# Routed experts in pairs of half-blocks, each on 64 columns of TensorE

## What is computed

```
logits = x @ router_w + router_b          # [1250, 8]
p, idx = top_k(softmax(logits), 2)        # two experts per node
for e in range(8):                        # w1[e]: [768, 1152], w2[e]: [1152, 768], all fp32
    h = gelu(x @ w1[e] + b1[e])
    y = h @ w2[e] + b2[e]
    out = out + y * gates[:, e:e+1]       # gate 0 where the node did not choose e
```

## Time and profile before

| | |
|---|---|
| median of the runs | 4152.34 µs |
| span of the profiled execution | 4146.1 µs |
| what lies around the span (median less span) | 6.2 µs |
| TensorE matmul busy | 3653.2 µs (88%) |
| DVE, ScalarE, GpSimd busy | 2328.8, 1499.3, 1303.8 µs |
| last stage, `route` | 3416.8 to 3467 µs |
| last stage, `experts` | 3467 to 4146 µs |

### The profile page before, as it was taken

One profiled execution on the slowest core, in us unless ns is written; L12 is line 12 of the kernel. 1 busy time (PEld: TensorE's weight loads), 2 busy tenths in 40 slices (PEclk: granted clock), 3 DMA queues, 4 the chain that ended last, 5 costly groups with the idle time before them and its releaser, 6 DMA issues. The chain is left out here.

```text
span 4146.1 us, 73449 instructions
## 1 busy us (share of the span) xinstructions
PE 3653.2 (88%) x18975; PEld 2492.1 (60%) x18976; DVE 2328.8 (56%) x8246; ACT 1499.3 (36%) x4487; POOL 1303.8 (31%) x1301
## 2 busy tenths in 40 slices
PE   6989999679999897898957779998989997999998
PEld 4656666444444465666646665444556775888787
DVE  5469999977777766777778885640232232101010
ACT  0047777557777421222246663320020100111111
POOL 0045555447777105666636651000000000011010
PEclk9999999879999999999979999999999998999999
DMA  3278888648888427888856761012600008426261
GB/s 117 78 216 268 263 268 269 209 142 268 266 264 270 154 76 248 274 273 273 273 190 196 197 183 70 0 46 91 263 1 27 27 8 325 154 53 248 46 217 58
DMA packets 190279, 711.89 MB, mean 172 GB/s; under 512 B 30132, under 2 KB 52580, under 8 KB 189812
## 3 DMA queue, kind: packets, MB, share of 16 engines
q0 software_dynamic: 102208, 486.37, 37.7%
q1 hardware_dynamic: 87796, 224.24, 15.7%
q10 hardware_dynamic: 192, 0.25, 0.0%
HBM read 777.87 MB, written 33.04 MB: 196 GB/s over the span
## 5 line engine op out<-in xcount | busy, mean ns | idle before, releaser
L635 POOL DMA_INDIRECT X<-fs,near_src x664 | 629.5, 948 | 869.1 <-POOLq L100 436.6
L699 PE MATMUL l_psZ<-X,ident 128*128 128x396 f32 (+3 forms) x2656 | 810.2, 427 | 7.0 <-DMA X<-fs,near_src 6.2
L699 PEld LDWEIGHTS l_psZ<-X,ident 128*128 128x128 f32 x2656 | 498.1, 190 | 195.1 <-DMA X<-fs,near_src 7.2
L696 PE MATMUL l_psZ<-fd,l_spread 128*128 x1328 | 448.9, 418 | 110.4 <-ACT l_spread L612 54.8
L985 PE MATMUL a_psO<-X,a_sel 128*128 128x396 f32 (+1 forms) x1328 | 463.4, 504 | 44.9 <-DVE X L939 44.3
L968 ACT ACTIVATE X<-X,L 128x99 f32<-128x99 f32 x1328 | 373.4, 364 | 131.2 <-DMA X<-fs,pair_src 122.0
L985 PEld LDWEIGHTS a_psO<-X,a_sel 128*128 128x128 f32 x1328 | 242.1, 190 | 265.7 <-issue 105.4
L923 POOL DMA_INDIRECT X<-fs,pair_src x324 | 353.8, 1092 | 139.2 <-issue 82.0
L696 PEld LDWEIGHTS l_psZ<-fd,l_spread 128*128 128x128 f32 x1328 | 234.7, 189 | 193.6 <-issue 173.5
L2522 PEld LDWEIGHTS r_psH<-r_rowsT,ew_w 128*128 128x128 f32 x2916 | 331.7, 193 | 8.4 <-issue 1.5
L662 DVE SCALAR_TENSOR_TENSOR l_zr<-l_psZ,l_attn 128x99 f32<-128x99 f32 x1660 | 330.6, 255 | 8.4 <-issue 6.0
(11 more groups left out here) (504 smaller groups left out, 5317.3 us busy)
## 6 DMA issues: line engine op xcount, KB each, us to landing
ew_w<-in_L_ffn_w SPq DMA_DIRECT2D x54, 3456.0 KB
dsts<-near_rows SPq DMA_DIRECT2D x166, 128.0 KB
room<-in_L_ffn_w SPq DMA_DIRECT2D x8, 2304.0 KB
hw_w<-in_L_ffn_w SPq DMA_DIRECT2D x24, 576.0 KB
X<-fs,near_src POOLq DMA_INDIRECT x664
H<-in_L_ffn_b SPq DMA_DIRECT2D x27, 384.0 KB
X<-in_x SPq DMA_DIRECT2D x2, 3456.0 KB
X<-fs,pair_src POOLq DMA_INDIRECT x332
```

The source lines that it names most:

```text
L635: nc.gpsimd.indirect_dma_start(out=g[:, n % RING, :], out_offset=None, in_=fs, in_offset=bass.IndirectOffsetOnAxis(ap=R.near_src[:, n:n + ...
L696: nc.tensor.matmul(psZ[k][:, a, 0:half], spread[:, j // 4, k, :], R.fd[:, ds(b, 1), lo:hi].squeeze(1), start=True, stop=True)
L699: last = nc.tensor.matmul(psZ[k][:, a, 0:hi - lo], R.ident[:], g[:, j, lo:hi], start=False, stop=True, skip_group_check=True)
```

## The change

Blocks are now half-blocks of 64 slots: MB = 46, and R.slots has MP = 23 columns, in which partitions 0 to 63 belong to half-block i (side 0) and partitions 64 to 127 to half-block i + 23 (side 1). So side 0 goes through half-blocks 0 to 22 and side 1 through 23 to 45, each with weight buffers, and fresh now means that a side's expert differs from that of its block before.

Both products take the rows, or the hidden values, as stationary operand, 64 columns per side, and the weights move: side 0 writes partitions 0 to 63 of PSUM and side 1 partitions 64 to 127, with the two sides' matmuls one after the other in program order. The hidden values thus come out with rows on partitions: DVE adds b1 (which is now loaded as broadcast rows per side), ScalarE applies gelu to the whole tile in one instruction, and nine transposes (`cross`) turn them for the second product. TensorE's order is inner(i), turn(i + 1), outer(i - 1), cross(i).

Each matrix is loaded in thirds with a semaphore each. SyncE's loop pass i waits for each third of inner(i), loads w1 of block i + 1 for both sides, then the bias, then waits for each third of outer(i) and loads w2, then waits for the addition and loads b2, now under the same condition. There are four register loads per pass.

`slots` has two more columns: the nodes with those of the other side replaced by a value out of range. GpSimd scatters each block in two indirect DMAs, one per side, and waits for each to land before the next, since a node may be on both sides. The loops of the other engines are written out.

The diff, cut to its core (indentation shortened by eight inside the scopes; the removed lines of `experts` are those of the kernel printed above):

```diff
-MB = (TOP * NODES - ME) // P + ME
-MSLOTS = MB * P
+SIDE = P // 2
+MB = (TOP * NODES - ME) // SIDE + ME
+MP = MB // 2
+assert MB == 2 * MP
+MSLOTS = MB * SIDE
 KH = MHID // P
+PARTS = 3
...
+    def load_first(self, sp, s, q, e, **how):
+        n = KD // PARTS
+        rows = self.w1[ds(e, 1)].squeeze(0).rearrange("(k p) h -> p k h", p=P)[:, q * n:(q + 1) * n, :]
+        sp.dma_start(self.first[s][:, q * n:(q + 1) * n, :], rows, **how).then_inc(self.s_first[s][q], 16)
+
+    def load_second(self, sp, s, q, e, **how):
+        n = KH // PARTS
+        rows = self.w2[ds(e, 1)].squeeze(0).rearrange("(k p) d -> p k d", p=P)[:, q * n:(q + 1) * n, :]
+        sp.dma_start(self.second[s][:, q * n:(q + 1) * n, :], rows, **how).then_inc(self.s_second[s][q], 16)
+
+    def load_bias(self, sp, s, e, **how):
+        sp.dma_start(self.bias[s * SIDE:(s + 1) * SIDE, :], self.b1[ds(e, 1)].squeeze(0).partition_broadcast(SIDE), **how).then_inc(self.s_bias, 16)
...
+    sp.wait_ge(s_mm, 3)
+    e = [sp.value_load(R.block_expert[0:1, s * MP:s * MP + 1], min_val=0, max_val=ME - 1) for s in range(2)]
+    for q in range(PARTS):
+        for s in range(2):
+            weights.load_first(sp, s, q, e[s])
+    for s in range(2):
+        weights.load_bias(sp, s, e[s])
+    for q in range(PARTS):
+        weights.load_second(sp, 0, q, e[0])
...
+    chain(nc.vector.tensor_scalar(side[:], block_of[:], float(MP), None, ALU.is_ge))
+    nc.vector.scalar_tensor_tensor(out=row_of[:], in0=side[:], scalar=float(SIDE), in1=row_of[:], op0=ALU.mult, op1=ALU.add)
+    chain(nc.vector.scalar_tensor_tensor(out=block_of[:], in0=side[:], scalar=-float(MP), in1=block_of[:], op0=ALU.mult, op1=ALU.add))
...
+    for s in range(2):
+        part = slice(s * SIDE, (s + 1) * SIDE)
+        nc.vector.tensor_scalar(R.slots[part, :, 2 + s], psS[part, 0], float(ROWS - 1), None, ALU.add)
...
-    load(0, 0, first=True)
-    load(0, 1)
-    with sp.Fori(0, PAIRS - 1) as i:
+    e = [expert(0, s) for s in range(2)]
+    for q in range(PARTS):
+        weights.load_second(sp, 1, q, e[1])
+    for s in range(2):
+        load_outer_bias(s, e[s])
+    with sp.Fori(0, MP - 1) as i:
+        e = [expert(i + 1, s) for s in range(2)]
+        fresh = [sp.value_load(R.block_fresh[0:1, ds(i + 1 + s * MP, 1)], min_val=0, max_val=1) for s in range(2)]
+        for q in range(PARTS):
+            sp.wait_ge(s_h, i * PARTS + q + 1)
+            for s in range(2):
+                weights.load_first(sp, s, q, e[s], cond=fresh[s], cond_hint=True)
+        sp.wait_ge(s_sum, i + 1)
         for s in range(2):
+            weights.load_bias(sp, s, e[s], cond=fresh[s], cond_hint=True)
+        for q in range(PARTS):
+            sp.wait_ge(s_y, i * PARTS + q + 1)
+            for s in range(2):
+                weights.load_second(sp, s, q, e[s], cond=fresh[s], cond_hint=True)
+        sp.wait_ge(s_add, i + 1)
+        for s in range(2):
+            load_outer_bias(s, e[s], cond=fresh[s], cond_hint=True)
...
+    def gather(i):
+        if i >= 2:
+            pool.wait_ge(s_turn, i - 1)
+        nc.gpsimd.indirect_dma_start(out=rows[i % 2], out_offset=None, in_=rows_table,
+                                     in_offset=bass.IndirectOffsetOnAxis(ap=R.slots[:, i, 0:1], axis=0)).then_inc(s_rows[i % 2], 16)
 
     gather(0)
     gather(1)
+    for i in range(MP):
+        if i:
             pool.sem_inc(s_landed, 1)
+        if i + 2 < MP:
+            gather(i + 2)
+        pool.wait_ge(s_scaled, i + 1)
+        for s in range(2):
+            nc.gpsimd.indirect_dma_start(out=out, out_offset=bass.IndirectOffsetOnAxis(ap=R.slots[:, i, 2 + s:3 + s], axis=0), in_=y[i % 2], in_offset=None,
+                                         bounds_check=NODES - 1, oob_is_err=False, compute_op=ALU.add).then_inc(s_put, 16)
+            pool.wait_ge(s_put, 32 * i + 16 * s + 16)
...
+    for i in range(MP):
+        act.wait_ge(s_sum, i + 1)
+        nc.scalar.activation(h[:], h[:], ACT.Gelu).then_inc(s_gelu, 1)
+        if i:
+            act.wait_ge(s_y, i * PARTS)
+        for q in range(PARTS):
+            act.wait_ge(s_cross, i * PARTS + q + 1)
+            n = KH // PARTS
+            nc.scalar.copy(hT[:, q * n:(q + 1) * n, :].rearrange("p k q -> p (k q)"), psT[:, q, 0:n * P]).then_inc(s_crossed, 1)
...
+    def add_inner(i):
+        dve.wait_ge(s_b1, 32 * (i + 1))
+        if i:
+            dve.wait_ge(s_cross, i * PARTS)
+        dve.wait_ge(s_h, (i + 1) * PARTS)
+        nc.vector.tensor_tensor(h[:], psH[:, :, 0:THIRD], b1t[:].rearrange("p (a d) -> p a d", a=PARTS), ALU.add).then_inc(s_sum, 1)
+
+    def finish(i):
+        dve.wait_ge(s_b2, 32 * (i + 1))
+        if i >= 2:
+            dve.wait_ge(s_landed, i - 1)
+        dve.wait_ge(s_y, (i + 1) * PARTS)
+        nc.vector.tensor_tensor(y[i % 2].rearrange("p (a d) -> p a d", a=2), psY[:, :, 0:HALF], b2t.rearrange("p (a d) -> p a d", a=2), ALU.add).then_inc(s_add, 1)
+        dve.wait_ge(s_add, i + 1)
+        nc.vector.tensor_scalar(y[i % 2], y[i % 2], R.slots[:, i, 1:2].bitcast(F32), None, ALU.mult).then_inc(s_scaled, 1)
...
+    def inner(i):
+        pe.wait_ge(s_turned, i + 1)
+        if i:
+            pe.wait_ge(s_sum, i)
+        for k in range(KD):
+            if k % (KD // PARTS) == 0:
+                for s in range(2):
+                    pe.wait_ge(s_w1[s][k * PARTS // KD], 16 * (i + 1))
+            for a in range(PARTS):
+                for s in range(2):
+                    last = nc.tensor.matmul(psH[sides[s], a, 0:THIRD], rowsT[:, k, sides[s]], w1t[s][:, k, a * THIRD:(a + 1) * THIRD],
+                                            start=(k == 0), stop=(k == KD - 1), skip_group_check=True)
+            if (k + 1) % (KD // PARTS) == 0:
+                last.then_inc(s_h, 1)
+
+    def cross(i):
+        pe.wait_ge(s_gelu, i + 1)
+        pe.wait_ge(s_turned, min(i + 2, MP))
         for m in range(KH):
+            last = nc.tensor.transpose(psT[:, m // 3, (m % 3) * P:(m % 3 + 1) * P], h[:, m // 3, (m % 3) * P:(m % 3 + 1) * P], R.ident[:])
+            if m % 3 == 2:
+                last.then_inc(s_cross, 1)
+
+    def outer(i):
+        pe.wait_ge(s_crossed, (i + 1) * PARTS)
+        if i:
+            pe.wait_ge(s_add, i)
         for m in range(KH):
+            if m % (KH // PARTS) == 0:
+                for s in range(2):
+                    pe.wait_ge(s_w2[s][m * PARTS // KH], 16 * (i + 1))
             for a in range(2):
+                for s in range(2):
+                    last = nc.tensor.matmul(psY[sides[s], a, 0:HALF], hT[:, m, sides[s]], w2t[s][:, m, a * HALF:(a + 1) * HALF],
+                                            start=(m == 0), stop=(m == KH - 1), skip_group_check=True)
+            if (m + 1) % (KH // PARTS) == 0:
+                last.then_inc(s_y, 1)
+
+    turn(0)
+    for i in range(MP):
+        inner(i)
+        if i + 1 < MP:
+            turn(i + 1)
+        if i:
+            outer(i - 1)
+        cross(i)
+    outer(MP - 1)
```

More of the change, by code:

```diff
@@ L2394, in experts @@
-        hT = [c.sb(f"hT{s}", [P, KH, P]) for s in range(2)]
-        psT = c.ps("psT", [P, 2, BANK])
-        psH = [c.ps(f"psH{j}", [P, BANK]) for j in range(4)]
+        b2t = R.H[:, 4, :]
+        rowsT = c.sb("rowsT", [P, KD, P])
+        h, hT = c.sb("h", [P, PARTS, THIRD]), c.sb("hT", [P, KH, P])
+        psH = c.ps("psH", [P, PARTS, BANK])
+        psT = c.ps("psT", [P, PARTS, BANK])
         psY = c.ps("psY", [P, 2, BANK])
-        s_b, s_bt, s_bc, s_turn, s_turned, s_h, s_gelu, s_y, s_add = (c.sem(x) for x in ("b", "bt", "bc", "turn", "turned", "h", "gelu", "y", "add"))
@@ L2399, in experts @@
-        s_b2, s_rows = ([c.sem(f"{x}{s}") for s in range(2)] for x in ("b2", "rows"))
+        s_turn, s_turned, s_h, s_sum, s_gelu, s_cross, s_crossed, s_y, s_add = (
+            c.sem(x) for x in ("turn", "turned", "h", "sum", "gelu", "cross", "crossed", "y", "add"))
+        s_b2, s_rows = c.sem("b2"), [c.sem(f"rows{s}") for s in range(2)]
         s_scaled, s_put, s_landed = (c.sem(x) for x in ("scaled", "put", "landed"))
+        sides = [slice(s * SIDE, (s + 1) * SIDE) for s in range(2)]
@@ L2512, in turn @@
                 last.then_inc(s_turn, 1)
-            def one(i, s, last_one=False):
-                j = i * 2 + s
-                pe.wait_ge(s_turned, j + 1)
-                pe.wait_ge(s_w1[s], i * 16 + 16)
-                for m in range(KH):
-                    if m >= 4:
-                        pe.wait_ge(s_gelu, j * KH + m - 3)
-                    for k in range(KD):
-                        last = nc.tensor.matmul(psH[m % 4][:, 0:P], w1t[s][:, k, m * P:(m + 1) * P], rowsT[s][:, k, :],
-                                                start=(k == 0), stop=(k == KD - 1))
-                    last.then_inc(s_h, 1)
-                if not last_one:
-                    turn(j + 1, 1 - s)
-                pe.wait_ge(s_w2[s], i * 16 + 16)
-                pe.wait_ge(s_add, j + 2)
+            def inner(i):
```

(6 more changed lines are left out.)

156 lines of the change are left out of this document (48 added, 108 removed).

## The result

| | before | after |
|---|---|---|
| median of the runs | 4152.76 µs (4 runs, 4151.53 to 4153.52) | 4292.72 µs (4 runs, 4289.36 to 4296.7) |
| span of the profiled execution | 4146.1 µs | 4288.7 µs |
| last stage: first transposes of `route` to the end | 729.3 µs | 866.2 µs |

The ratio is 1.0337 [1.0323, 1.0352]: slower, by 140 µs. The forecast was 4238 µs with a range of 4195 to 4300. The stages ahead of the last one are the same code and took 5.7 µs more in this trace; in a second pair of traces they took 4.3 µs less, while the last stage grew by 136.5 instead of 136.9. So the change costs 137 µs in its own stage, where the forecast had 86. The other 3 to 4 µs of the medians' 140 are not placed; the stages ahead, as these figures show, differ by more than that from run to run.

A forecast was written before the change was run, and what follows sets the result against it. TensorE's own work bounds the last stage; the change adds waits on SyncE, weights and gather. Start to 3524.1, fifteen quiet blocks 453, six fresh 207.6, ending 4213.7, clock 18, 6.2 to the median: 4238 µs (4195 to 4300).

The forecast's parts named there:

- rival 2: Scatter chain longer: full rounds of 6.3 µs and skipped-load semaphores at 1.6, blocks of 32.2 and 37, total 4282 µs; 18%.
- Pairs: TensorE's products: matmuls of the two sides overlap on two column halves, a pair costing one record, 23.2 µs per block.
- rival 4: TensorE's paired matmuls do not overlap: 23.2 µs more per block, total 4700 µs; 3%.
- The start: From `route` to inner(0): longer DVE list 0.9 and SyncE's held barrier 3, so inner(0) at 3480.9.
- Inner(0) to the end of outer(0): First block: inner(0) from 3480.9, inner(1) at 3499.8 with its weights covered at the start, outer(0) over at 3524.1.
- The announcement: TensorE waits each block for SyncE to announce inner's weights: inner at E + 5.3 (E: outer's end), 4.1 µs of stop.
- Rival 1: SyncE's announcement comes within cross, so TensorE alone bounds blocks at 25.4 µs, total 4093, or 4100 to 4130; 5%.
- The clock: Gaps before inner lower TensorE's granted clock: 12 µs for six long gaps, 6 for fifteen short ones, 18 together.
- Fresh weights: Six blocks where a side changes expert wait for w1's first third: inner at E + 9.9, blocks of 34.6 µs.
- The scatters: GpSimd's gather behind two scatter rounds of 5.3 µs: turn at E + 17.6, inner over at E + 17.05, chains nearly meeting.
- Quiet blocks: Blocks without new weights: 17.6 + 0.8 (turn, switch) + 11.8 = 30.2 µs each, fifteen of them 453.
- Rival 3: Only SyncE's chain holds TensorE, with no clock loss: blocks of 29.6 µs, total 4211 µs; 15%.

The follow-up runs named there:

- e1: Changed kernel with SyncE announcing w1 and b1 of block i + 1 ahead of its waits on outer(i - 1); ratio to the kernel before 1.036, +140.9 µs.
- e2: Changed kernel with GpSimd issuing gather(i + 3) ahead of block i's scatters, instead of gather(i + 2) behind block i - 1's; ratio to before 1.0346, +138.1 µs.
- e3: Changed kernel with both the edits of e1 and e2; ratio to the kernel before 0.9876, −50.1 µs.
- e4: e2 plus 36 unused identity transposes behind each cross, to keep TensorE busy in the stop before inner; ratio to the kernel before 1.0274, +105.7 µs.
- e5: e2 with SyncE's passes written out and the next pass's four register loads ahead of the waits on outer; ratio to the kernel before 1.0097, +42.3 µs.
- e7: e1 with only the first of each block's two scatters, leaving side 1's rows out of the result; ratio to the kernel before 0.9908, −34.9 µs.

## Why the prediction was right, and where its sizes were off

The mechanism was right in its parts. That the time came out 55 µs above the forecast is two terms, the clock and the scatter rounds, each too small in the forecast. They run side by side, and each alone would have made about half of the difference in quiet blocks or more (worked out below). The stated range holds the result only because rival 2 stretched it, by a price (a skipped load's semaphore at 1.6 µs) that is not paid, beside one (rounds of 6.3) that is right. That part is luck.

- **Pairs.** Predicted 23.2 + 0.14 for 72 + 72 records; 72 take 11.83 with the switch. Right; rival 4 falls.
- **The start.** `route` to inner(0): predicted 64.1, measured 64.15. Right in sum, by luck in its parts: the 3.9 stood for a longer list and a held barrier, but the first gather starts only 2.0 later than in the kernel before (53.7 after 51.7 from the start of `route`), and its rows are turned 7.9 µs behind it instead of 5.9.
- **Inner(0) to the end of outer(0).** 49.95 instead of 43.2. Missed: inner(1) waits 5.45 µs for its own w1, which the prediction held to be covered at the start, and runs 14.17 long.
- **The announcement.** E + 5.3 predicted, E + 5.85 measured, in the order and for the reasons given; the 0.55 is spread over the register loads (0.65 each instead of 0.6) and what stands ahead of them. The semaphore of a skipped load was taken at 0, and of the prediction's bounds that end is right: the first issue is at 3848.71, and inner starts at 3849.27, 0.56 µs later. The Trainium skill ("DMA: Bandwidth & Descriptors", Anatomy of one DMA) gives about 2 µs of fixed cost for a DMA on GpSimd's path, most of it the confirmation that the data has landed. The prediction's alternative laid that on SyncE's skipped loads; for a DMA whose condition is false the trace does not show it (0.56 µs). Rival 1 (the announcement is within cross) falls.
- **The clock: the term most out of size.** "Of the fifteen gaps of 4.1 I give one in five", and 18 µs in all. Every one of the fifteen lost it, at 1.4 to 3.0 µs: 32.1 µs where the forecast had 6. The six behind fresh weights lost 10.8 where it had 12, and inner(1), which it had not counted, 2.3. Together 45.3 µs, as much as the prediction's own upper end. A gap of 3 µs at 1.00 and one of 6 µs at 0.50 bound it from both sides, and the forecast took the side of the shorter; the gap came out at 4.7 instead of 4.1, nearer to the longer.
- **Fresh weights.** Inner at E + 9.9 predicted; E + 12.1, 13.2, 12.1, 12.4, 12.7 and 11.7 measured. In the first of them (E + 12.1, block 2) 1 µs is a later issue (E + 6.0), and 1.3 a slower first third (6.1 µs from issue to product instead of 4.8). What slows it was not tried. The six sum to 230.6 µs instead of 218.8 with their clock.
- **The scatters.** 5.3 a round predicted, 6.2 and 6.4 measured (3845.96, 3852.14, 3858.51): the upper bound. Most rounds of quiet blocks lie between 5.8 and 6.5. That is rival 2's price, but it hardly shows as a wait, as inner, slowed by the clock, ends about when the gather lands (3858.51 + 4.2 = 3862.7, and turn at 3862.63). That the two chains "nearly meet" was right, and e1, e2 and e3 show it.
- **What each of the two is worth.** e4 takes the clock's loss away with the stop left in place, but in a kernel whose gather is early. There quiet blocks fall to 30.26. In the kernel after, the gather would still hold turn until E + 18.7 to 19.4 (e1's quiet blocks), where inner at the full clock is over at E + 17.6. With 0.8 for turn and 11.8 for outer that makes blocks of 31.3 to 32.0, an estimate, against 32.6 measured in the mean and 30.2 forecast. So the clock on top of the late gather costs about 1 µs a block, the late gather on top of the clock nothing (e2). The sizes of both had to be right for the forecast to come out.
- **Quiet blocks.** 30.6 with their share of clock, 32.6 measured: over fifteen blocks that is 30.5 of the missing 51.
- **The end.** A second scatter for 5.3, measured 7.6: the round is 6.15, and from the last scatter's start to the end it is 9.7 instead of 8.4, which was not followed up.

The missing 51.3 µs of the stage: 6.8 behind inner(0), 30.5 in quiet blocks, 11.8 in fresh ones, 2.3 at the end. Rival 3 (no clock loss, 4211) falls with the clock's term. The prediction's own sums have small slips that change nothing: its terms put inner(1) at 3499.6 and not 3499.8, and fresh inner at E + 9.8 and not 9.9; twenty-one times 2.1 is 44, not 45.

## What to carry to other kernels

Before a loop is split or reordered, write down for each engine which wait its queue holds ahead of the thing that the bottleneck needs next: here one announcement behind a wait for the product before, and one gather behind two scatters, turned a gain of 50 µs into a loss of 140. When two such chains run side by side, taking away one shows nothing; take away both before the idea is given up. And price a new stop of a few µs ahead of a matmul with the clock that it loses, not by its length alone.

## What the hardware showed that was not expected

- A stop of 4.7 µs after nine transposes lost the granted clock in every block (0.50 for about 3 µs of work), one of 1.6 to 2.0 µs in none (e5). Between these the length alone does not decide: three stops of 3.0 to 3.4 in front of turn all lost it (e7, outer behind them 13.3 to 14.0 µs, granted clock 0.50 to 0.56 for 2 to 3 µs), where the gap at 62 µs in the kernel before, 3.3 long, kept it at 1.00. What else decides was not tried. Inner's lengths of 13.4 and 14.5 µs alternate with whole blocks of 31.9 and 33.0; why was not tried.
- A DMA whose condition is false costs SyncE 0.3 µs of queue (six in 1.98) and its semaphore was there within 0.56 µs of the first issue.
- An accumulating scatter of which half the rows are out of range and dropped takes as long as the full one: mostly 5.8 to 6.5 µs in quiet blocks, against 6.3.
- Four register loads by SyncE cost 2.6 µs (the first starts at 3845.9, the last at 3847.8 and is done with 0.65 later), more than the nine transposes beside which they run (1.20).
